# A recurrent two-layer kernel: the exponentials' stream placed 34 units, instead of 40, behind the stream of row maxima

## The reference

```
attn = q_lat @ c_kv.T / sqrt(hs);  attn = where(causal, attn, -inf)
attn = softmax(attn)               # exp(attn - rowmax) / sum
y    = attn @ c_kv
```

## Time and profile before

| | us |
|---|---|
| median of 3 runs (lowest, highest) | 609.96 (602.48, 612.54) |
| time of the profiled execution | 606.47 |
| its span, first to last instruction | 604.7 |
| PE busy | 573.6 (95%) |
| DVE busy | 392.3 (65%) |
| ACT busy | 352.2 (58%) |
| POOL busy | 176.8 (29%) |

### The profile page before, as it was taken

How to read it: one execution, slowest core, us unless ns; L and a number is a source line. 1 busy time by engine, 2 the same in 40 slices (tenths; PEclk the granted TensorE clock), 3 DMA queues, 4 the chain that set the end, 5 groups by cost and what they waited for, 6 DMA issues and landing times.

```text
span 604.7 us, 17394 instructions
## 1 busy us (share of the span) xinstructions
PE 573.6 (95%) x7233; PEld 383.4 (63%) x7233; DVE 392.3 (65%) x975; ACT 352.2 (58%) x678; POOL 176.8 (29%) x351
## 2 busy tenths in 40 slices
PE   7799999898999999999999999999999999799897
PEld 3345575466666785667666776677677777555465
DVE  3478767666768776776867776867767676412553
ACT  3412556864658656765667466865676476576231
POOL 6256204221215322341415212532224201311221
PEclk9999999999999999999999999999999999999999
DMA  3766193749054202620153204420262000000001
GB/s 92 165 155 132 32 105 70 135 92 101 24 122 81 63 4 79 144 60 4 51 114 61 62 12 109 104 63 3 63 130 54 22 12 1 27 18 3 2 4 35
DMA packets 58161, 39.41 MB, mean 65 GB/s; under 512 B 17956, under 2 KB 57987, under 8 KB 58083
## 3 DMA queue, kind: packets, MB, share of 16 engines
q1 hardware_dynamic: 58051, 38.29, 31.2%
q10 hardware_dynamic: 32, 0.01, 0.0%
HBM read 24.46 MB, written 9.96 MB: 57 GB/s over the span
## 4 chain that ended last, share of the span: by engine, by line
PE 80%; ACT 9%; DVE 5%; issue 2%; DMA 1%; POOL 1%; SPq 0%; DVEq 0%; POOLq 0%
PE ps_s L944 12%; PE ps_v L963 12%; PE ps_e L925 7%; PE ps_a L879 5%; PE ps_c L1028 4%; PE ps_a L865 4%; PE ps_e L917 3%; PE ps_e L921 3%; PE ps_e L747 3%; PE ps_a L829 3%; PE ps_s L947 3%; ACT hid L1248 2%; PE ps_a L844 2%; ACT prob L1265 2%; PE ps_c L1010 2%
## 5 line engine op out<-in xcount | busy, mean ns | idle before, releaser
L1480 DVE TENSOR_REDUCE cand<-ps_s 128x4 f32<-128x512 f32 (+1 forms) x320 | 213.1, 686 | 65.5 <-PE ps_s L947 45.9
L1265 ACT ACTIVATE prob<-ps_e 128x512 f32<-128x512 f32 x320 | 187.0, 598 | 79.1 <-PE ps_e L925 53.9
L944 PE MATMUL ps_s<-kst,qst 72*128 72x128 bf16 (+2 forms) x1024 | 124.8, 234 | 5.2 <-DMA kst<-k_scratch 2.0
L944 PEld LDWEIGHTS ps_s<-kst,qst 72*128 72x128 bf16 (+1 forms) x1024 | 74.0, 98 | 66.0 <-DVE cand L1480 29.6
L925 PE MATMUL ps_e<-qst,kst 75*128 75x256 bf16 (+3 forms) x416 | 104.2, 281 | 0.0
L963 PE MATMUL ps_v<-prob,vaug 128*32 128x512 f32 (+3 forms) x1024 | 87.1, 441 | 0.0
L917 PE MATMUL ps_e<-identb,negmask 128*128 128x150 bf16 (+3 forms) x320 | 72.5, 226 | 4.1 <-ACT prob L1265 4.0
L921 PE MATMUL ps_e<-qst,kst 128*128 128x128 bf16 x384 | 73.9, 219 | 0.0
L747 PE MATMUL ps_e<-identb 128*128 128x512 bf16 x115 | 41.1, 413 | 1.9 <-POOL identb L521 1.9
L925 PEld LDWEIGHTS ps_e<-qst,kst 75*128 75x128 bf16 x416 | 40.5, 97 | 3.5
L947 PE MATMUL ps_s<-negmask,identb 128*128 128x300 bf16 (+1 forms) x128 | 40.8, 319 | 0.0
(11 more groups left out here) (344 smaller groups left out, 913.0 us busy)
## 6 DMA issues: line engine op xcount, KB each, us to landing
qst<-q_scratch SPq DMA_DIRECT2D x48, 192.0 KB
kst<-k_scratch SPq DMA_DIRECT2D x48, 192.0 KB
q_scratch<-qparts SPq DMA_DIRECT2D x24, 128.0 KB, 2.3
k_scratch<-kparts SPq DMA_DIRECT2D x24, 128.0 KB, 2.3
x_res<-in_L_attn_x_dram SPq DMA_DIRECT2D x8, 256.0 KB, 3.2
xn<-in_L_attn_x_dram SPq DMA_DIRECT2D x7, 256.0 KB, 3.5
out_dram<-second SPq DMA_DIRECT2D x7, 256.0 KB, 2.5
max_scratch<-mrow SPq DMA_DIRECT2D x16, 96.0 KB, 1.8
```

Source lines behind the costliest of these rows:

```text
L944: last = mm(ps_s[:, bank, w * n:w * (n + 1)], q[0:rows, hd, tok(i)], k[0:rows, hd, keys[0]:keys[1]], start=(n == 0), stop=True, skip_group ...
L1265: af(prob[:, u, :], ps_e[:, u % 2, :], ACT.Exp).then_inc(S["e_emptied"], 1)
L1480: vec.tensor_reduce(cand[:, i, h0:h0 + FILLS * (len(hds) - 1) + 1:FILLS, S_SLOT[u]], ps_s[:, u % 2, :].rearrange("p (a c) -> p a c", a=len ...
```

## The change

The E stream follows the S stream by `LEAD = 34` units instead of 40. With 40, an iteration's S units are units 0 to 39 of `nxt`. With 34, the first iteration issues only S units 0 to 33 (and 34 fillers instead of 40), and each later iteration issues, at its unit positions 0 to 5, S units 34 to 39 of `cur`, and at positions 6 to 39 S units 0 to 33 of `nxt`. In the ninth iteration the first six positions hold S units 34 to 39 of sequence 7.

Pieces move with it. In `PLAN`: `m_parts0` from (2,0) to (2,5); `m_rows0` from (2,4) to (3,0), where it stands just before `h2`; `stacks0` from (3,0) to (3,1); `m_parts1` from (4,0) to (0,5) of the following iteration, for `cur`. In `LAST_PLAN`, `m_parts1` comes in at (0,5), ahead of `ln2_rstd` and `hn_norm`. In `FIRST_PLAN`, `m_rows0`, `prepare4`, `v` and `v_out` come one unit earlier and `stacks1` moves from (0,4) to (2,3), behind `m_rows0`. The wait for `masks_ready` 2 moves from `settle` to a new `settle_second` after the second iteration; `settle` keeps a wait for `masks_ready` 1. DVE's wait for `nm_ready` is now made at the start of groups 0 and 2.

```diff
 PLAN = {
-    (0, 0): ["c_u3"], (0, 2): [...], (0, 4): ["h1", "ln2_rstd", "hn_norm"],
+    (0, 0): ["c_u3"], (0, 2): [...], (0, 4): ["h1", "ln2_rstd", "hn_norm"], (0, 5): ["m_parts1"],
...
-    (1, 9): [...], (2, 0): ["ln1_stats", "lev_d2", "ln1_rstd", "m_parts0"], ...
+    (1, 9): [...], (2, 0): ["ln1_stats", "lev_d2", "ln1_rstd"], ...
-    (2, 4): ["yt", "m_rows0"], (2, 5): ["lev_a4", "xnt"], (2, 6): ["pv0", "q", "lev_d4"], ...
-    (2, 9): [...], (3, 0): ["stacks0", "h2", "low_blocks"], (3, 1): ["lev_a6"], ...
+    (2, 4): ["yt"], (2, 5): ["lev_a4", "xnt", "m_parts0"], (2, 6): ["pv0", "q", "lev_d4"], ...
+    (2, 9): [...], (3, 0): ["m_rows0", "h2", "low_blocks"], (3, 1): ["lev_a6", "stacks0"], ...
-    (3, 9): ["c_u2", "pv1"], (4, 0): ["m_parts1", "gelu", "stacks1"], ...
+    (3, 9): ["c_u2", "pv1"], (4, 0): ["gelu", "stacks1"], ...
 LAST_PLAN = {
-    (0, 5): ["ln2_rstd", "hn_norm"], (0, 6): ["pv0", "gb2"], (0, 8): ["gb3"], ...
+    (0, 5): ["m_parts1", "ln2_rstd", "hn_norm"], (0, 6): ["pv0", "gb2"], (0, 8): ["gb3"], ...
 FIRST_PLAN = {
-    (0, 0): ["xnt"], (0, 2): ["q"], (0, 4): ["k", "stacks0", "stacks1"], ...
-    (2, 0): ["m_parts0"], (2, 2): ["prepare4"], (2, 4): ["m_rows0"], (2, 5): ["masks2"], (3, 2): ["v"], (3, 4): ["v_out"], (4, 0): ["m_parts1"],
+    (0, 0): ["xnt"], (0, 2): ["q"], (0, 4): ["k", "stacks0"], ...
+    (2, 0): ["m_parts0"], (2, 1): ["prepare4"], (2, 3): ["m_rows0", "stacks1"], (2, 5): ["masks2"], (3, 1): ["v"], (3, 3): ["v_out"],
...
+LEAD = 34
...
             if step < GROUPS:
-                yield "unit", (cur, nxt, step, u)
+                at = UNITS * step + u
+                if cur is None:
+                    if at < LEAD:
+                        yield "unit", (None, 0, u, nxt, step, u)
+                else:
+                    whose, ahead = (cur, at + LEAD) if at + LEAD < GROUPS * UNITS else (nxt, at + LEAD - GROUPS * UNITS)
+                    yield "unit", (cur, step, u, whose, ahead // UNITS, ahead % UNITS)
...
     for t in range(2, SEQUENCES):
         yield from iteration(*(seqs[t - behind] if t >= behind else None for behind in range(5)))
+        if t == 2:
+            yield "settle_second", ()
...
             def settle():
-                pe.wait_ge(S["masks_ready"], 2)
+                pe.wait_ge(S["masks_ready"], 1)
                 pe.wait_ge(S["ones_loaded"], 32)
                 ready(PREP_OUT)
+
+            def settle_second():
+                pe.wait_ge(S["masks_ready"], 2)
...
-                if mgrp == 0 and u == 0:
-                    after(dve, S["nm_ready"], nxt.count(2, 0))
+                if mgrp % 2 == 0 and u == 0:
+                    after(dve, S["nm_ready"], nxt.count(2, mgrp // 2 - 1))
```

More of the change, by code:

```diff
@@ L92 @@
 FIRST_PLAN = {
-    (0, 0): ["xnt"], (0, 2): ["q"], (0, 4): ["k", "stacks0", "stacks1"], (0, 7): ["gt"], (1, 2): ["masks"], (1, 6): ["prepare2"], (1, 9): ["prepare3"],
-    (2, 0): ["m_parts0"], (2, 2): ["prepare4"], (2, 4): ["m_rows0"], (2, 5): ["masks2"], (3, 2): ["v"], (3, 4): ["v_out"], (4, 0): ["m_parts1"],
+    (0, 0): ["xnt"], (0, 2): ["q"], (0, 4): ["k", "stacks0"], (0, 7): ["gt"], (1, 2): ["masks"], (1, 6): ["prepare2"], (1, 9): ["prepare3"],
+    (2, 0): ["m_parts0"], (2, 1): ["prepare4"], (2, 3): ["m_rows0", "stacks1"], (2, 5): ["masks2"], (3, 1): ["v"], (3, 3): ["v_out"],
 }
@@ L97 @@
 PLAN_SECOND = ("load_x", "ln1_stats", "ln1_rstd", "ln1_norm", "xnt", "q", "k", "stacks0", "stacks1")
-PLAN_NEXT = ("rn", "vl0", "vl1", "route", "v_out", "logits", "gates", "gate_norm", "gt", "h0", "h1", "h2", "h3", "gelu", "v", "m_parts0", "m_rows0", "m_parts1")
+PLAN_NEXT = ("rn", "vl0", "vl1", "route", "v_out", "logits", "gates", "gate_norm", "gt", "h0", "h1", "h2", "h3", "gelu", "v", "m_parts0", "m_rows0")
 PLAN_OLDER = ("c_u3", "c_y3", "c_out")
-PLAN_CURRENT = ("gb0", "gb1", "gb2", "gb3", "out", "pv0", "pv1", "pv2", "yt", "x1", "m_rows1", "zero_state")
+PLAN_CURRENT = ("gb0", "gb1", "gb2", "gb3", "out", "pv0", "pv1", "pv2", "yt", "x1", "m_parts1", "m_rows1", "zero_state")
 SEQUENCES = 8
+LEAD = 34
 class SecondLayer:
@@ L890, in m_rows, with unit @@
                 last.then_inc(S["a_filled"], 1)
-            def unit(cur, nxt, grp, u):
-                if nxt is not None:
-                    s_unit(nxt, grp, u)
+            def unit(cur, grp, u, ahead, ahead_grp, ahead_u):
+                if ahead is not None:
+                    s_unit(ahead, ahead_grp, ahead_u)
                 if cur is not None:
@@ L1143, in _ @@
             run(pieces | {"unit": unit, "weights": weights, "prepare": prepare, "prepare2": prepare2, "prepare3": prepare3, "prepare4": prepare4,
-                          "settle": settle, "weight_k": weight_k, "busy": before_maxima, "fill": keep_busy})
+                          "settle": settle, "settle_second": settle_second, "weight_k": weight_k, "busy": before_maxima, "fill": keep_busy})
         @block.scalar
@@ L1367, in settle, with settle_second @@
             def settle():
+                dve.wait_ge(S["masks_ready"], 1)
+                dve.wait_ge(S["prep_out"], PREP_OUT)
+            def settle_second():
                 dve.wait_ge(S["masks_ready"], 2)
-                dve.wait_ge(S["prep_out"], PREP_OUT)
             def a_full(b, n):
@@ L1470, in out_piece, with unit @@
                                          in1=ps_a[:, :], op0=ALU.add, op1=ALU.mult).then_inc(S["a_emptied"], 1)
-            def unit(cur, nxt, mgrp, u):
+            def unit(cur, grp, at, nxt, mgrp, u):
                 if nxt is None:
@@ L1630, in _ @@
                 pieces[f"lev_a{lv}"] = lambda b, lv=lv: lev_a(b, lv)
-            run(pieces | {"unit": unit, "prepare": prepare, "settle": settle, "busy": before_maxima})
+            run(pieces | {"unit": unit, "prepare": prepare, "settle": settle, "settle_second": settle_second, "busy": before_maxima})
 PREP_OUT = 18
```

## The result

| | before | changed |
|---|---|---|
| median of the runs, us | 607.61 (602.48 to 612.54, 4 runs) | 623.28 (621.03 to 625.37, 4 runs) |
| ratio, 95% interval | | 1.0289 [1.0238, 1.0341] |
| profiled execution / its span, us | 606.5 / 604.7 | 622.3 / 620.6 |
| gelu to gelu, iterations four to seven, mean, us | 66.27 | 68.35 |
| last gelu to the end, us | 93.67 | 101.62 |

The kernel became 2.9% slower; a second measurement of the same kernel gave 1.0233 [1.0194, 1.0273]. The forecast was 618 with a range of 606 to 626, most of it on "within 2%". The range held; the likeliest class did not.

What follows compares the result with a forecast made beforehand. PE, busy 95% of the span, was taken as the bound. Terms -3.95 - 0.5 + 7.7 + 3.1 + 4.3 = +10.7 us gave execution 617.1, or 620.6 on the median's scale; it said 618, range 606 to 626.

Steps and rivals of the forecast that it cites:

- within 2%: Outcome class for the whole kernel: a time within about 12 us of no change, given a chance of 0.60.
- First iteration, -3.95: Six S units fewer there: the stretch from unit 34 to the second iteration vanishes, -3.95 us if the maxima arrive in time.
- m_rows0 at (3,0), 7 x 1.10: Directly before h2, PE waits for ACT's copy of the shared bank: 1.10 us in iterations two to eight, +7.7 us.
- the transposes themselves, which are only moved: At (3,0), 0.23 of the 1.32 us from transposes to h2 was counted as moved work, leaving 1.10 as cost.
- Second iteration, -0.5: At (2,4), PE's 0.53 us wait for POOL's parts goes because m_rows0 leaves: -0.5 us.
- Masks, 6 x 0.39 and 6 x 0.13: Masked S units leave positions 0 to 3, lengthening waits at E unit (0,2) and vl0: +2.3 and +0.8 us.
- The table load's drain: A skill's rule of about 1380 ns drain per ACT table load would make the first part near -2.9 us; not adopted.
- The third iteration's stacks, 0: PE's 1.09 us wait at an S unit, read as stacks0's load, goes into the wait for ACT: 0, bound -1.1.
- Ninth iteration, +4.3: Added reductions on DVE and m_parts1 on POOL delay hn_norm and then gb3 on PE: +4.3 us, bounds 1.4 and 5.
- The head, 0: Head and first 34 units of the first iteration: no difference predicted, 0 us.
- ACT being late at (3,0): Rival: an extra exponential of 0.60 us before the mrow copy, seven times, 4.2 us; execution 621.4, chance 0.10.
- slower by 2%: Outcome class for the whole kernel, slower by over 2%: chance 0.37, including 0.20 as a third of the forecast.

Runs made afterwards that it cites:

- distance 30: Changed kernel with LEAD = 30 instead of 34 and the m_parts, m_rows and stacks0 pieces moved to match: median 626.54 us, ratio 1.0301 to the kernel before.
- POOL's order: Changed kernel with ln2_rstd ahead of m_parts1 at (0,5) in the ninth iteration: median 617.37 us, ratio 1.0143 to the kernel before.
- the kernel with dummies: Changed kernel with 19 dummy products on PE in the ninth iteration, where it waits for hn_norm: median 618.91 us, ratio 1.0183 to the kernel before.
- the one with m_rows0 earlier: Changed kernel with m_rows0 moved from (3,0) to (2,9), behind pv1: median 615.36 us, ratio 1.0128 to the kernel before.

## Why the prediction was right and where it was wrong

The places and the direction were right, the sum too small: +15.8 us in the profile against +10.7, and by stretches that the change touches +19.4. Of the missing 8.7 us some 5 are the clock.

*First iteration, -3.95.* Right, and its condition too: the last memset of the masks runs at 57.41 in the changed kernel, 2.9 us behind the start of the second iteration, so the moved wait was needed, and the maxima were in time.

*m_rows0 at (3,0), 7 x 1.10.* Right in place and mechanism: seven waits of 0.93 us, 6.5 in all. The price was too small: 1.42 when put into the kernel before. The term that failed is "the transposes themselves, which are only moved": at (2,4) they had run in time that DVE needed, so nothing came back there. With the 0.1 us in h2 that is 0.32 us an iteration, some 2.2 us in all.

*Second iteration, -0.5.* The wait for POOL's parts is gone, and in the kernel before with m_rows0 moved the half us shows. In the changed kernel it is eaten up: PE waits 0.53 and 0.85 us for two reductions, 1.38 us where it was 0.44, and the iteration is 1.66 us longer instead of 0.6.

```profile
87.36 0.40 PE L956 MATMUL ps_s<-kst,qst 72*128 72x128 bf16 x4 [0.85 <-DVE cand L1495]
```

*Masks, 6 x 0.39 and 6 x 0.13.* Right in sign and size. At the head of a steady iteration (0,2) waits 0.27 us more and L1124 0.18 that wasn't there, 0.45 together; vl0 waits 0.13 more. At distance 30, with the masks back, all three are as before: 0.24, nothing, 0.17. No run moved the masks alone.

*The table load's drain.* Not there: the exponential starts 252.97 - 251.68 = 1.29 us behind its load again, as in the earlier trace rows, the second iteration's S stream starts without a wait, and the first part came out at -3.95, not at the -2.9 of that rule.

*The third iteration's stacks, 0.* The wait of 1.09 us went and ACT's took its place, 1.02 us at 112.91; that it had been the load of stacks0 isn't shown, for the profile names no cause for it. With 0.81 us for yT (as before) and 0.51 us for a reduction just ahead, it is followed by a half clock of 3.4 us. I predicted +1.6 for this iteration; it was +3.6, and a half-clock stretch is worth 1.5 to 1.6 of it. All six profiles with distance 34 have this stretch, none of the other six has it.

*Ninth iteration, +4.3.* The chain grew by 4.43 us: right. The step failed in "+4.3" being all: the sum had PE's time at one speed. PE's standing still brought 13.65 us of half clock, +3.5 us behind gb3. Of the chain POOL's order alone is 2.7 us.

*The head, 0.* -3.56 us lies in code that the change doesn't touch: the first S unit started at 25.75 instead of 27.71, and the 34 units from there took 28.72 instead of 30.32 us, since before had a half clock for 3.4 us there. The other profile of the changed kernel has the late start and the half clock. So against its own start the profiled change cost +19.4 us, not +15.8; the medians, over several heads, say +15.7 and +13.4. The twelve profiles sort the half clock of the head: it follows in the nine in which PE waited 1.87 to 2.72 us for the first stack of keys, and not in the three with 1.46 to 1.65. Why that wait differs stays open.

*The scale.* The profiled execution before was a good one: its mean granted clock is 0.997, while the median of the 48 executions of that kernel beside the experiments is 0.994. So a comparison of the two profiles makes the clock's part larger than it is in the medians.

*The range and the chances.* The 618 is 2.6 us below the 620.6 of the prediction's own working, without a reason. That 623.28 lies within 606 to 626 is in part luck: the upper bound was made for ACT being late at (3,0), which didn't happen, and it gave room for the clock, which was in no term. The sum was 1.3 us under the 2% line with two terms open that could only add. I gave slower by 2% a third of the forecast's own case; with costs on one side it should have had half.

## What to carry to other kernels

A shorter distance between producer and consumer saves at the ends of a pipeline once, and pays in every period wherever a moved piece lands beside one that shares its buffer or its engine's queue: here 3.95 us against 1.4 us in each of seven iterations, and 3.2 us in each of five in my own first try at distance 30. Walk a moved piece along every queue on which it has a part, and ask at its old place whose slack it was. When a new wait is priced, price the clock after it as well.

## What the runs showed of the hardware

- TensorE's granted clock fell to 0.5 at places where PE stood still, but not each time. In five profiles PE waited 1.72 us at the same S unit of the ninth iteration: behind it the clock fell in two (after 1.6 and 1.3 us), in two only at the wait of 3.5 us for gb3, in one not at all. A wait of 1.59 us was followed by a fall in two profiles of three, waits of 3.23 us in eight cases of ten, and waits of 0.41 and 0.95 us close together in one (the kernel before with m_rows0 moved, 525.12 us). A wait of 1.64 us (1.63 in one) in the second layer's last part, in all twelve profiles, was followed by none. Where DVE and POOL were left alone and only PE was kept at work, it didn't fall.
- What a fall costs depends on how full PE is behind it. A stretch of 3.4 us cost 1.5 to 1.6 us on a full PE, and 0.3 to 0.8 in the ninth iteration ahead of gb3. 13.65 and 10.24 us cost 3.5 both times: 8.9 and 9.0 us of them lie behind gb3, and the rest ran while PE waited for others.
- In the third iteration PE stood for 1.89 us at 148.84 with nothing that it waited for in the profile (1.70 at 151.38 before); in the kernel with dummies it is 0.09 and in the one with m_rows0 earlier 0.29. It comes and goes without an edit near it. With the head and the number of half-clock stretches it is what differs between two executions of one kernel; which of them weighs most no run separates.
